# Attention and mixture of experts on one core: the scattered rows of six of the eight batches take a way through DRAM, the root of the variance moves ahead of the weights' low halves, and batch 0's scatters lose their pacing

## The chip, the core and the metric

The kernel runs on one core of a Trainium2 chip. The metric is the device time of one execution in microseconds (us). A core has five instruction streams that run side by side and wait for each other through semaphores: TensorE (PE in the profile; PEld is its loading of weights), VectorE (DVE), ScalarE (ACT), GpSimd (POOL) and SyncE (SP, which only issues transfers here). ACT and POOL issue transfers too. Sixteen DMA engines move the data.

## The reference

4096 tokens of 256 values, in 8 batches of 512. Each row is normalised, and two branches start from the normalised rows `xn`:

```
xn  = (x - mean) / sqrt(var + 1e-5)
# attention over channels, per batch
q, k, v = xn Wq, xn Wk, xn Wv
s   = softmax(q^T k / sqrt(8)) applied to v^T, transposed, times Wo
# mixture of experts, per token
scores  = softmax(xn gate^T)                 # 32 experts in 8 groups
chosen  = 6 best experts in the 3 best groups, weights normalised to 1
routed  = sum over chosen of weight_e * (silu(xn w1_e^T) * (xn w3_e^T)) w2_e^T
shared  = (silu(xn sw1^T) * (xn sw3^T)) sw2^T
out = x + s * silu(routed + shared)
```

## The kernel before

**Two phases.** The first goes over the 8 batches (B = 8). A batch is 4 tiles of 128 rows (TB = 4). For each it computes the attention branch (by the Gram matrix `xn^T xn`), the shared expert, the gate's scores, the choice of experts and the place of every row in a list sorted by expert, and it scatters the rows. The second phase takes the sorted list as 112 pairs of pages of 128 rows (PAIRS), runs the experts over them, stores the results into the same list, gathers 6 rows for each token, adds them up with their weights and writes the output.

**The list.** `slots_d` in DRAM, one row of 1 KB per (token, chosen expert). Its pages are first filled with zeros ("pads"): SP writes those that batch b can reach in `s_pads[b]` (4 smaller ones for batch 0, `s_first_pads[t]`), 3 MB each. Before the rows are scattered they are split in a high and a low half-precision half. ACT writes the high halves (`split_high`, L539), DVE the low ones (`split_low`, L995, semaphore `s_split`). The result is `split[b % 2]`, a ring of two tiles of one batch each, one in `early`, one in `work`.

**The scatters.** POOL scatters batch b with 24 indirect DMAs (4 tiles of rows, 6 chosen experts each; L487) of 128 rows. It needs the places (`s_slots`, DVE L989 at the end of `place`), the pads and the split rows. Their landing is counted in `s_disp[b % 2]`, and `split_high(b)` waits for the count of batch b - 2, as both use one tile. Ahead of some scatters POOL also waits for a count of PE's work (`let_pass`, L466 to L482): in each batch b ahead of scatter 2 for the gate's scores of batch b + 1 (`s_lg_ps`), ahead of 4 for the first half of the shared output (`s_y_ps`), 7 for the attention's product with Wo (`s_r_ps`), 9 for the second half (`s_y_ps`), 11 for the product with Wv (`s_m_ps`), 13 for the counts of rows per expert (`s_cnt`), 15 for the attention's output (`s_at_ps`), and 17, 19 and 21 for work of batch b + 1 (`s_ab_ps`, `s_a_ps`, and `s_xt_ps`, the transposes of batch b + 2 where there is one). No data needs these waits.

**The other streams in batch b.** Each runs its order as written out in `batch(b)`. PE: shared expert up, two products of the attention, transposes and gate of b + 1, softmax times Wo (L710), second half of the shared output (L726), product with Wv (L710), Gram matrix of b + 1 (L732), counts (L704, L705), attention output (L726). ACT: copies PSUM to SBUF between those; of note, after the shared output's copies and the store of `ysh_d` (L604) it normalises the first half of batch b + 2 (`normal`, L527), then copies the product with Wv (L610), then normalises the second half. `normal` needs `shift` and `rstd` from DVE. DVE: softmax's maximum, `spread_of(b + 2)` (mean and variance), `route(b + 1)` (choice of experts), `split_low(b + 1)`, `low_weights(b - 1)` (low halves of four experts' weights, 12 instructions of L1050), `spread_root(b + 2)` and `moved_mean` (L887 to L898, which give `rstd` and `shift`), `place(b + 1)`, `weigh(b + 1)`. The standard deviation that `spread_root` starts from was computed on ACT (L519) earlier in the batch.

**SP.** It loads x, loads of the batches ahead interleaved with the pads, each ahead of a wait for the choice of experts of an earlier batch (`s_sel`). Then it loads the last weights (L376), and then the pairs' rows (L403, L407), stores of results, and so on. The first 14 pairs (EARLY) may be loaded before all rows are scattered: `full_pairs` on DVE finds which pages no later batch can still reach after batch 6; SP loads those once the scatters of batches 0 to 6 have landed.

Of the kernel before, what the change touches and what calls it, by code (L numbers as in the profile page):

```python
# [7 lines left out]
ALU = mybir.AluOpType  # L8
# [43 lines left out]
EARLY = 14  # L52
# [41 lines left out]
def gated_attention_moe(nc, x, wq, wk_, wvT, wo, gwT, wexp, sw13T, sw2T, out):  # L94
    with ExitStack() as ctx:
# [12 lines left out]
        ysh_d = nc.dram_tensor("ysh_d", [T, H], F32).ap()  # L108

        x_b, ysh_b = (a.rearrange("(b t p) c -> b p t c", t=TB, p=P) for a in (x, ysh_d))  # L110
        x_t, ysh_t, out_t = (a.rearrange("(t p) c -> t p c", p=P) for a in (x, ysh_d, out))
# [42 lines left out]
        split = [v.rearrange("p (t c) -> p t c", t=TB) for v in (split_0, part(4608, 1024))]  # L154
        split16 = [v.bitcast(F16).rearrange("p (t s c) -> p t s c", t=TB, s=2) for v in (split_0, part(4608, 1024))]
# [113 lines left out]
        s_disp = sems("s_disp", XN_RING)  # L269
# [70 lines left out]
        def _(sp):  # L340
# [18 lines left out]
            for b in range(1, B):  # L359
                to = (b + 1) * BATCH_ROWS + E  # L360
                if b >= 2:
                    sp.wait_ge(s_sel, b - 1)
                if 3 <= b + 1 < B:
                    load_x(b + 1)
                sp.dma_start(slots_d[at * P:to * P].rearrange("(n p) c -> p n c", p=P),
                             pad[:].unsqueeze(1).to_broadcast([P, to - at, H])).then_inc(s_pads[b], 16)
                at = to

# [9 lines left out]
            sp.wait_ge(s_disp[0], 16 * BATCH_ROWS * (B // 2))  # L378
            sp.wait_ge(s_disp[1], 16 * BATCH_ROWS * (B // 2 - 1))
# [64 lines left out]
        def _(pool):  # L444
# [30 lines left out]

            for b in range(B):
# [14 lines left out]
            for k in range(XN_RING):  # L491
                pool.wait_ge(s_disp[k], 16 * BATCH_ROWS * (B // XN_RING))
# [21 lines left out]
        def _(act):  # L514
# [20 lines left out]
            def split_high(b):  # L535
                act.wait_ge(s_xn, b * TB + TB)
                if b >= XN_RING:
                    act.wait_ge(s_disp[b % XN_RING], 16 * BATCH_ROWS * (b // XN_RING))
                act.activation(split16[b % XN_RING][:, :, 0, :], xn[b % XN_RING], ACT.Copy, scale=X_UP).then_inc(s_split_hi, 1)  # L539
# [30 lines left out]
            def batch(b):  # L570
# [33 lines left out]
                act.dma_start(ysh_b[b], y_s).then_inc(s_ysh[b % 2], 16)  # L604
                if last:
# [259 lines left out]
        def _(dve):  # L865
# [126 lines left out]
            def split_low(b, tiles=range(TB)):  # L992
                dve.wait_ge(s_split_hi, b + 1)
                for t in tiles:
                    dve.scalar_tensor_tensor(split16[b % XN_RING][:, t, 1, :], xn[b % XN_RING][:, t], X_UP,  # L995
                                             split16[b % XN_RING][:, t, 0, :], ALU.mult, ALU.subtract).then_inc(s_split, 1)
# [67 lines left out]
            def batch(b):  # L1064
# [10 lines left out]
                elif b + 2 == B:  # L1075
# [125 lines left out]
```

## Time and profile before

| | |
|---|---|
| median of 3 runs | 686.68 us (683.47 to 690.63) |
| profiled execution, its own time | 691.99 us |
| its span, first to last instruction | 690.2 us |
| mean granted TensorE clock | 0.922 of full speed |
| PE busy | 548.6 us, 79% |
| POOL busy | 383.4 us, 56% |
| scatters (L487) | 192, from 28.7 to 317.7 us |
| gathers (L508) | 192, the first at 369.8 us |

The time outside of the span is 1.8 us. A busy share says how long an engine had an instruction in work; whether its idle time matters is read from who waits for it. In a row of the timeline the bracket says how long the engine was idle before the instruction and what released it: an instruction of another engine, "issue" (nothing that the profile shows), or "remote" (a semaphore whose sender the profile does not name). The ends of matmuls are modelled, so a signal that reaches its receivers long after the matmul's end is seen only from the receivers' rows.

### The profile page before, as it was taken

The numbers are of one execution on the slowest core, as the hardware profiler recorded it, in microseconds if no ns is written. First come the engines' busy times: TensorE is split into PE (matmuls) and PEld (weight loads), VectorE is DVE, ScalarE is ACT, GpSimd is POOL, SyncE is SP. The second block draws the span as 40 slices with busy tenths as digits, with TensorE's granted clock in tenths as the row PEclk, the third lists the DMA queues.
The fourth block names the chain that finished last, engine by engine and source line by source line (L and its number), as shares of the span: only waits on it lengthen the run. The fifth ranks groups of instructions, "written<-read, shape, count | busy, mean of one in ns | idle before, by whom it ended". The sixth has DMA issues, their size and how long they took to land.

```text
span 690.2 us, 14473 instructions
## 1 busy us (share of the span) xinstructions
PE 548.6 (79%) x4095; PEld 446.7 (65%) x4095; DVE 472.2 (68%) x1443; ACT 359.1 (52%) x606; POOL 383.4 (56%) x402
## 2 busy tenths in 40 slices
PE   7789696979697978437999889888888889888830
PEld 6566575756576765326999777777777777677620
DVE  6968687877788877722454567667677667667765
ACT  5546464546464644224655656556556556556421
POOL 1156667676666766753003556556565556565662
PEclk9889798998898999868999999999999999999975
DMA  9999996858393532754888888888888988888764
GB/s 320 416 354 347 366 334 227 285 214 298 130 334 113 207 117 91 230 150 122 201 217 262 290 280 283 280 280 285 290 272 292 279 279 267 290 276 286 226 198 141
DMA packets 111288, 174.80 MB, mean 253 GB/s; under 512 B 25072, under 2 KB 68848, under 8 KB 110320
## 3 DMA queue, kind: packets, MB, share of 16 engines
q1 hardware_dynamic: 87280, 108.29, 47.4%
q0 software_dynamic: 18432, 50.36, 23.2%
q10 hardware_dynamic: 5504, 15.24, 6.4%
q8 instruction: 40, 0.66, 0.4%
q14 instruction: 32, 0.26, 0.1%
HBM read 78.41 MB, written 92.27 MB: 247 GB/s over the span
## 4 chain that ended last, share of the span: by engine, by line
PE 53%; DVE 21%; issue 15%; another core or an unknown queue 6%; ACT 4%; DMA 1%; DVEq 0%; SPq 0%; ACTq 0%
PE ps L835 17%; PE ps L857 8%; PE ps L726 7%; PE ps L710 6%; PE ps L818 6%; PE ps L718 4%; DVE sw L1133 3%; PE ps L845 3%; PE ps L732 2%; DVE w_all L1050 2%; DVE work L1152 2%; DVE work L1159 1%; DVE stats L877 1%; DVE early L1141 1%
## 5 line engine op out<-in xcount | busy, mean ns | idle before, releaser
L508 POOL DMA_INDIRECT early<-slots_d,slot_at x192 | 186.6, 972 | 178.0 <-DMA slots_d<-early 56.6
L487 POOL DMA_INDIRECT slots_d<-early,slot_at x96 | 96.9, 1009 | 75.0 <-issue 25.7
L487 POOL DMA_INDIRECT slots_d<-work,slot_at x96 | 97.7, 1018 | 45.1 <-issue 26.5
L835 PE MATMUL ps<-w_all,xnT 128*128 x798 | 102.9, 275 | 15.9 <-issue 13.6
L835 PEld LDWEIGHTS ps<-w_all,xnT 128*128 128x128 f16 x798 | 71.4, 98 | 36.3 <-issue 24.6
L647 ACT ACTIVATE xnT<-ps 128x1024 f16<-128x1024 f16 x67 | 68.8, 1029 | 46.6 <-PE ps L818 28.0
L668 ACT ACTIVATE early<-ps 128x512 f32<-128x512 f32 x112 | 67.3, 602 | 46.6 <-remote 30.8
L818 PE MATMUL ps<-ident,work 128*128 128x128 f16 x796 | 66.7, 222 | 24.9 <-issue 24.8
L1159 DVE CAST work<-ps 128x256 f16<-128x256 f32 x75 | 31.6, 422 | 75.0 <-remote 45.0
L1133 DVE SCALAR_TENSOR_TENSOR sw<-early,wk,sw 128x256 f32<-128x256 f32 x160 | 77.7, 486 | 3.5
L818 PEld LDWEIGHTS ps<-ident,work 128*128 128x128 f16 x796 | 54.6, 99 | 28.8 <-issue 26.4
L653 ACT ACTIVATE work<-ps 128x256 f32<-128x256 f32 x112 | 43.9, 393 | 55.6 <-remote 37.9
L857 PE MATMUL ps<-w_all,work 128*128 x447 | 62.6, 277 | 0.9 <-issue 0.9
L1152 DVE SCALAR_TENSOR_TENSOR work<-ps,work 128x256 f32<-128x256 f32 x112 | 46.5, 416 | 20.4 <-ACT work L653 19.0
L710 PE MATMUL ps<-early,work 128*128 128x256 f32 x128 | 39.4, 462 | 25.8 <-ACT work L533 18.9
L835 PE MATMUL ps<-w_all,sw 128*128 x396 | 50.6, 274 | 8.3 <-issue 8.0
L710 PEld LDWEIGHTS ps<-early,work 128*128 128x128 f32 x128 | 28.6, 231 | 34.7 <-ACT work L533 21.0
L726 PE MATMUL ps<-work,early 128*128 128x256 f32 x128 | 34.7, 432 | 17.7 <-issue 13.8
L857 PEld LDWEIGHTS ps<-w_all,work 128*128 128x128 f16 x447 | 43.9, 99 | 6.3 <-issue 1.5
L835 PEld LDWEIGHTS ps<-w_all,sw 128*128 128x128 f16 x396 | 35.4, 98 | 18.6 <-issue 12.7
L647 ACT ACTIVATE sw<-ps 128x1024 f16<-128x1024 f16 x33 | 34.0, 1032 | 20.9 <-remote 15.4
L718 PE MATMUL ps<-xnT,sw 128*128 128x512 f16 x192 | 44.0, 379 | 0.0
(164 smaller groups left out, 989.4 us busy)
## 6 DMA issues: line engine op xcount, KB each, us to landing
slots_d<-early SPq DMA_DIRECT2D x112, 256.0 KB
work<-slots_d SPq DMA_DIRECT2D x100, 256.0 KB
slots_d<-pad SPq DMA_DIRECT2D x7, 3072.0 KB
w_all<-in_wexp ACTq DMA_DIRECT2D x7, 1536.0 KB
slots_d<-work SPq DMA_DIRECT2D x1, 5120.0 KB, 19.2
s_all<-in_x SPq DMA_DIRECT2D x8, 512.0 KB, 6.3
ysh_d<-work ACTq DMA_DIRECT2D x8, 512.0 KB
early<-ysh_d SPq DMA_DIRECT2D x32, 128.0 KB
```

Of the source, the lines that this page charges most:

```text
L487: pool.indirect_dma_start(slots_d[:, :], bass.IndirectOffsetOnAxis(ap=slot_at[:, at:at + 1], axis=0), split[b % XN_RING][:, t, :], None).t ...
L508: pool.indirect_dma_start(gath[:, at % GATH_RING, :], None, slots_d[:, :], bass.IndirectOffsetOnAxis(ap=slot_at[:, rank_of(at):rank_of(at) ...
L647: act.activation(x_halves[n % 3], turned_pair(p), ACT.Copy).then_inc(s_eT, 1)
L668: act.activation(y_e[:, p % DEEP, :], ps[:, 2 + p % 2, :], ACT.Copy, scale=1.0 / W_UP).then_inc(s_ey, 1)
L710: mm = pe.matmul(ps[:, bank, m * H:(m + 1) * H], lhs[:, k, m * P:(m + 1) * P], rhs[:, k, :], start=(k == 0), stop=(k == HC - 1))
L718: mm = pe.matmul(ps[:, 4 + 2 * m + w, :], sw13[:, w_low, w, k, m * P:(m + 1) * P], xnT16[:, x_low, k, :], start=(n == 0 and k == 0), stop= ...
L726: mm = pe.matmul(ps[:, bank + n, t * H:(t + 1) * H], lhs[:, k, at:at + P], rhs[:, k, :], start=(k == 0), stop=(k == HC - 1))
L818: mm = pe.transpose(turned_pair(p)[:, at:at + P], slot16[:, at_slot(p) + h, low, c * P:(c + 1) * P], ident16[:])
L835: mm = pe.matmul(ps[:, 5 + p % 2, h * 2 * I:(h + 1) * 2 * I], turned_x(p)[:, x_low * HC + k, h * P:(h + 1) * P], w16[:, bass.ds(at + (w_lo ...
L857: mm = pe.matmul(ps[:, 2 + p % 2, h * H:(h + 1) * H], hT_e[p % 3][:, h_low, h, :], w16[:, bass.ds(at + (w_low * WEXP + HC * 2 * I), H)], s ...
L1133: dve.scalar_tensor_tensor(acc[:, k, :], gath[:, at % GATH_RING, :], wk[:, rank_of(at):rank_of(at) + 1], ysh_l[k] if at % TOP_K == 0 else ...
L1152: dve.scalar_tensor_tensor(h_e[p % 2], up(p)[:, :, 1, :], 1.0 / (X_UP * W_UP), silu_e[p % 2], ALU.mult, ALU.mult).then_inc(s_eh, 1)
```

## The change

- **Rows through DRAM.** `split` gets a tile per batch: batch 0's is `passing`, the 4 KB per partition in `work`, those of batches 1 to 7 are all one tile in `early`. For batches 1 to 6 ACT stores the split rows to a new DRAM tensor `rows_d` (after the store of `ysh_d`), SP loads them tile by tile into `passing` as soon as that tile's scatters of the batch before have landed, and POOL scatters from `passing`. Batch 0 is scattered from `passing` directly, batch 7 from its own tile in `early`. `s_disp` is now counted per tile of rows, 4 semaphores in place of 2. `split_high(b)` waits for the store of batch b - 1 in place of the scatters of batch b - 2.
- **SP's order.** x of batches 3 and 4 ahead of the pads of batch 1, then per batch: the next x, the pads, the four loads of `passing`. The waits for `s_sel` are gone; what holds SP back is `s_rows` and `s_disp`.
- **Batch 0's scatters** wait for no count of PE's work.
- **DVE's order.** `spread_root(b + 2)` and `moved_mean` ahead of `low_weights(b - 1)`.
- **Early pairs.** Found after batch 5 in place of 6, 22 pairs in place of 14; SP may load them once batches 0 to 5 have landed.

```diff
-EARLY = 14
+EARLY, EARLY_BATCHES = 22, 6
...
-        split = [v.rearrange("p (t c) -> p t c", t=TB) for v in (split_0, part(4608, 1024))]
...
+        passing = part(4608, 1024, TB)
+        split_at = [part(4608, 1024)] + [split_0] * (B - 1)
+        split = [v.rearrange("p (t c) -> p t c", t=TB) for v in split_at]
...
             for b in range(1, B):
                 to = (b + 1) * BATCH_ROWS + E
-                if b >= 2:
-                    sp.wait_ge(s_sel, b - 1)
-                if 3 <= b + 1 < B:
-                    load_x(b + 1)
+                for n in (3, 4) if b == 1 else (b + 3,):
+                    if n < B:
+                        load_x(n)
                 sp.dma_start(slots_d[at * P:to * P].rearrange("(n p) c -> p n c", p=P),
                              pad[:].unsqueeze(1).to_broadcast([P, to - at, H])).then_inc(s_pads[b], 16)
                 at = to
+                if b < B - 1:
+                    sp.wait_ge(s_rows[b], 16)
+                    for t in range(TB):
+                        sp.wait_ge(s_disp[t], 16 * TOP_K * b)
+                        sp.dma_start(passing[:, t, :], rows_t[b * TB + t]).then_inc(s_passing[t], 16)
...
-            sp.wait_ge(s_disp[0], 16 * BATCH_ROWS * (B // 2))
-            sp.wait_ge(s_disp[1], 16 * BATCH_ROWS * (B // 2 - 1))
+            for t in range(TB):
+                sp.wait_ge(s_disp[t], 16 * TOP_K * EARLY_BATCHES)
...
-                if n in due:
+                if b >= 1 and n in due:
                     pool.wait_ge(*due[n])
...
-                    pool.wait_ge(s_split, b * TB + t + 1)
+                    if b == 0 or b == B - 1:
+                        pool.wait_ge(s_split, b * TB + t + 1)
+                    else:
+                        pool.wait_ge(s_passing[t], 16 * b)
...
                         pool.indirect_dma_start(slots_d[:, :], bass.IndirectOffsetOnAxis(ap=slot_at[:, at:at + 1], axis=0),
-                                                split[b % XN_RING][:, t, :], None).then_inc(s_disp[b % XN_RING], 16)
+                                                passing[:, t, :] if b < B - 1 else split[b][:, t, :], None
+                                                ).then_inc(s_disp[t], 16)
...
-                if b >= XN_RING:
-                    act.wait_ge(s_disp[b % XN_RING], 16 * BATCH_ROWS * (b // XN_RING))
+                if b >= 2:
+                    act.wait_ge(s_rows[b - 1], 16)
...
                 act.dma_start(ysh_b[b], y_s).then_inc(s_ysh[b % 2], 16)
+                if b + 2 < B:
+                    act.wait_ge(s_split, (b + 2) * TB)
+                    act.dma_start(rows_b[b + 1], split[b + 1]).then_inc(s_rows[b + 1], 16)
...
-                elif b + 2 == B:
+                if b + 1 == EARLY_BATCHES:
                     full_pairs()
...
                 split_low(b + 1)
-                if b >= 1:
-                    low_weights(b - 1)
                 if b + 2 < B:
                     spread_root(b + 2)
                     moved_mean()
+                if b >= 1:
+                    low_weights(b - 1)
                 place(b + 1)
```

POOL, the first scatters of batch 0 (the waits are for PE's gate of batch 1, shared output and product with Wo). Before:

```order
L487 DMA slots_d<-early,slot_at 28672x256 [waits s_first_pads0,s_split,s_slots]
L487 DMA slots_d<-early,slot_at 28672x256
L487 DMA slots_d<-early,slot_at 28672x256 [waits s_lg_ps]
L487 DMA slots_d<-early,slot_at 28672x256
L487 DMA slots_d<-early,slot_at 28672x256 [waits s_y_ps]
L487 DMA slots_d<-early,slot_at 28672x256
L487 DMA slots_d<-early,slot_at 28672x256 [waits s_first_pads1,s_split]
L487 DMA slots_d<-early,slot_at 28672x256 [waits s_r_ps]
L487 DMA slots_d<-early,slot_at 28672x256
L487 DMA slots_d<-early,slot_at 28672x256 [waits s_y_ps]
```

And now:

```order
L498 DMA slots_d<-work,slot_at 28672x256 [waits s_first_pads0,s_split,s_slots]
L498 DMA slots_d<-work,slot_at 28672x256 x5
L498 DMA slots_d<-work,slot_at 28672x256 [waits s_first_pads1,s_split]
L498 DMA slots_d<-work,slot_at 28672x256 x5
L498 DMA slots_d<-work,slot_at 28672x256 [waits s_first_pads2,s_split]
L498 DMA slots_d<-work,slot_at 28672x256 x5
```

Of the waits only those for the pads and for the split rows of a tile stay; in batch 0 the ten waits of `let_pass` are gone, and the source is in `work`.

DVE, in batch 2, from the low halves of batch 3's rows to the counts. Before:

```order
L995 SCALAR_TENSOR_TENSOR work<-early,work 128x256 [waits s_split_hi]
L995 SCALAR_TENSOR_TENSOR work<-early,work 128x256 x3
L1050 SCALAR_TENSOR_TENSOR w_all<-w_all 128x256 [waits s_whi]
L1050 SCALAR_TENSOR_TENSOR w_all<-w_all 128x256 x11
L887 RECIPROCAL rough<-std 128x4 [waits s_std]
L888 SCALAR_TENSOR_TENSOR newt<-rough 128x4 [waits s_chain]
L889 SCALAR_TENSOR_TENSOR newt<-mv,newt 128x4 [waits s_chain]
L890 SCALAR_TENSOR_TENSOR rstd<-newt,rough 128x4 [waits s_chain]
L898 SCALAR_TENSOR_TENSOR shift<-mv,rstd 128x4 [waits s_chain]
L947 MEMSET early 128x32
L949 COPY counts<-ps 128x4x32 [waits s_cnt]
```

And now (L1010 is the low halves, L1065 the weights', L902 to L913 root and shift, L964 the counts):

```order
L1010 SCALAR_TENSOR_TENSOR early<-early 128x256 [waits s_split_hi]
L1010 SCALAR_TENSOR_TENSOR early<-early 128x256 x3
L902 RECIPROCAL rough<-std 128x4 [waits s_std]
L903 SCALAR_TENSOR_TENSOR newt<-rough 128x4 [waits s_chain]
L904 SCALAR_TENSOR_TENSOR newt<-mv,newt 128x4 [waits s_chain]
L905 SCALAR_TENSOR_TENSOR rstd<-newt,rough 128x4 [waits s_chain]
L913 SCALAR_TENSOR_TENSOR shift<-mv,rstd 128x4 [waits s_chain]
L1065 SCALAR_TENSOR_TENSOR w_all<-w_all 128x256 [waits s_whi]
L1065 SCALAR_TENSOR_TENSOR w_all<-w_all 128x256 x11
L962 MEMSET early 128x32
L964 COPY counts<-ps 128x4x32 [waits s_cnt]
```

The five small instructions that give `shift` come ahead of the twelve for the weights.

SP, from the pads of batch 1 to the x that goes with batch 3. Before:

```order
L365 DMA slots_d<-pad 128x24x256 [waits s_const]
L342 DMA s_all<-in_x 128x4x256 [waits s_sel]
L365 DMA slots_d<-pad 128x24x256
L342 DMA s_all<-in_x 128x4x256 [waits s_sel]
L365 DMA slots_d<-pad 128x24x256
L342 DMA s_all<-in_x 128x4x256 [waits s_sel]
```

And now:

```order
L346 DMA s_all<-in_x 128x4x256 [waits s_const]
L346 DMA s_all<-in_x 128x4x256
L368 DMA slots_d<-pad 128x24x256
L375 DMA work<-rows_d 128x256 [waits s_disp0,s_rows1]
L375 DMA work<-rows_d 128x256 [waits s_disp1]
L375 DMA work<-rows_d 128x256 [waits s_disp2]
L375 DMA work<-rows_d 128x256 [waits s_disp3]
L346 DMA s_all<-in_x 128x4x256
L368 DMA slots_d<-pad 128x24x256
L375 DMA work<-rows_d 128x256 [waits s_disp0,s_rows2]
```

The pads of batch 2 stand behind four loads that wait for batch 0's scatters, and those of batch 3 behind the loads that wait for batch 1's.

## Rows read from the trace of the kernel before

**Rows 1.** Windows from POOL's first scatter of a batch to the next's: length, busy times, clock, DMA.
```profile
28.70:68.50 39.80, 33.83 (x151) 26.95 (x152) 32.01 (x119) 21.32 (x37) 23.88 (x24) 0.86 1.03 358
...
246.00:281.00 35.00, 28.44 (x114) 21.15 (x115) 27.47 (x98) 15.32 (x24) 24.13 (x24) 0.90 0.39 137
```
**Rows 2.** Timeline of POOL: scatters of batches 0, 1 and 2.
```profile
28.69 1.42 POOL L487 DMA_INDIRECT slots_d<-early,slot_at  x1 [25.64 <-DVE slot_at L989]
...
68.52 0.96 POOL L487 DMA_INDIRECT slots_d<-work,slot_at  x1 [0.30 <-issue]
...
79.16 1.73 POOL L487 DMA_INDIRECT slots_d<-work,slot_at  x1 [1.96 <-remote]
...
100.19 0.96 POOL L487 DMA_INDIRECT slots_d<-work,slot_at  x1 [1.27 <-PE ps L685]
...
103.98 0.96 POOL L487 DMA_INDIRECT slots_d<-early,slot_at  x1 [0.30 <-issue]
```
**Rows 3.** Timeline of DVE: places of batch 1; low weights, shift of batch 5.
```profile
58.80 0.18 DVE L989 TENSOR_TENSOR slot_at<-in_order,in_page 128x24 int32<-128x24 int32 x1
...
147.00 4.10 DVE L1050 SCALAR_TENSOR_TENSOR w_all<-w_all 128x256 f16<-128x256 f32 x12
...
154.04 0.16 DVE L898 SCALAR_TENSOR_TENSOR shift<-mv,rstd 128x4 f32<-128x4 f32 x1 [0.54 <-DVE rstd L890]
```
**Rows 4.** Timeline of PE: product with Wv in batch 1; attention output, batches 3 and 4.
```profile
73.32 1.89 PE L726 MATMUL ps<-early,work 128*128 128x256 f32 x8
79.56 3.78 PE L710 MATMUL ps<-work,early 128*128 128x256 f32 x8 [4.36 <-issue]
...
156.84 6.74 PE L726 MATMUL ps<-work,early 128*128 128x256 f32 x16 [3.61 <-ACT work L610]
...
194.19 3.72 PE L726 MATMUL ps<-work,early 128*128 128x256 f32 x16 [0.26 <-ACT work L610]
```
**Rows 5.** Timeline of ACT: batch 0, then the signals that came late, batches 1 to 7.
```profile
43.98 0.60 ACT L602 ACTIVATE work<-ps 128x512 f32<-128x512 f32 x1 [2.15 <-PE ps L710]
...
46.34 0.38 ACTq L604 DMA_DIRECT2D ysh_d<-work  x1
...
47.84 0.57 ACT L610 ACTIVATE work<-ps 128x512 f32<-128x512 f32 x1
...
78.91 0.60 ACT L602 ACTIVATE work<-ps 128x512 f32<-128x512 f32 x1 [3.87 <-remote]
...
156.19 0.60 ACT L610 ACTIVATE work<-ps 128x512 f32<-128x512 f32 x1 [0.36 <-remote]
...
292.00 0.60 ACT L598 ACTIVATE work<-ps 128x512 f32<-128x512 f32 x1 [10.13 <-remote]
```
**Rows 6.** Waits, by length: first 320 to 369 us, then 375 to 650 us.
```profile
DVE work L1159 <- PE ps L845: 16.6, 14, 1.9
...
DVE work L1159 <- remote: 42.6, 23, 4.0
```
**Rows 7.** Timeline of POOL: the last two waits ahead of the one at 292 us.
```profile
272.08 0.96 POOL L487 DMA_INDIRECT slots_d<-early,slot_at  x1 [1.84 <-remote]
...
298.07 0.95 POOL L487 DMA_INDIRECT slots_d<-work,slot_at  x1 [3.38 <-remote]
```
**Rows 8.** DMA issues: KB each, us to landing; 60 to 130 us, then whole span.
```profile
s_all<-in_x SPq DMA_DIRECT2D x2, 512.0 KB, 10.1
...
s_all<-in_x SPq DMA_DIRECT2D x8, 512.0 KB, 6.3
...
slots_d<-work SPq DMA_DIRECT2D x2, 512.0 KB, 19.8
```
**Rows 9.** Timeline of PE: last attention output, then the first pair of pages.
```profile
298.48 5.90 PE L726 MATMUL ps<-work,early 128*128 128x256 f32 x16 [13.80 <-issue]
...
312.21 1.86 PE L818 MATMUL ps<-ident,work 128*128 128x128 f16 x16 [7.72 <-issue]
```

More of the change, by code:

```diff
@@ L108, in gated_attention_moe @@
         ysh_d = nc.dram_tensor("ysh_d", [T, H], F32).ap()
-        x_b, ysh_b = (a.rearrange("(b t p) c -> b p t c", t=TB, p=P) for a in (x, ysh_d))
-        x_t, ysh_t, out_t = (a.rearrange("(t p) c -> t p c", p=P) for a in (x, ysh_d, out))
+        rows_d = nc.dram_tensor("rows_d", [T, H], F32).ap()
+        x_b, ysh_b, rows_b = (a.rearrange("(b t p) c -> b p t c", t=TB, p=P) for a in (x, ysh_d, rows_d))
+        x_t, ysh_t, out_t, rows_t = (a.rearrange("(t p) c -> t p c", p=P) for a in (x, ysh_d, out, rows_d))
         w_all = sb("w_all", [P, E * WEXP])
@@ L153, in gated_attention_moe @@
         y_s = part(3584, 1024, TB)
-        split = [v.rearrange("p (t c) -> p t c", t=TB) for v in (split_0, part(4608, 1024))]
-        split16 = [v.bitcast(F16).rearrange("p (t s c) -> p t s c", t=TB, s=2) for v in (split_0, part(4608, 1024))]
+        passing = part(4608, 1024, TB)
+        split_at = [part(4608, 1024)] + [split_0] * (B - 1)
+        split = [v.rearrange("p (t c) -> p t c", t=TB) for v in split_at]
+        split16 = [v.bitcast(F16).rearrange("p (t s c) -> p t s c", t=TB, s=2) for v in split_at]
         mx, nmx, rsum, rinv = (sb(n, [P, HC]) for n in ("mx", "nmx", "rsum", "rinv"))
@@ L268, in gated_attention_moe @@
         s_split_hi, s_split = sem("s_split_hi"), sem("s_split")
-        s_disp = sems("s_disp", XN_RING)
+        s_disp = sems("s_disp", TB)
+        s_rows, s_passing = sems("s_rows", B), sems("s_passing", TB)
         s_g_ps, s_a_ps, s_s_ps, s_r_ps, s_m_ps = (sem(f"s_{n}_ps") for n in "gasrm")
@@ L487, in _ @@
                         pool.indirect_dma_start(slots_d[:, :], bass.IndirectOffsetOnAxis(ap=slot_at[:, at:at + 1], axis=0),
-                                                split[b % XN_RING][:, t, :], None).then_inc(s_disp[b % XN_RING], 16)
-            for k in range(XN_RING):
-                pool.wait_ge(s_disp[k], 16 * BATCH_ROWS * (B // XN_RING))
+                                                passing[:, t, :] if b < B - 1 else split[b][:, t, :], None
+                                                ).then_inc(s_disp[t], 16)
+            for t in range(TB):
+                pool.wait_ge(s_disp[t], 16 * TOP_K * B)
             pool.sem_inc(s_scattered, 1)
@@ L536, in split_high @@
                 act.wait_ge(s_xn, b * TB + TB)
-                if b >= XN_RING:
-                    act.wait_ge(s_disp[b % XN_RING], 16 * BATCH_ROWS * (b // XN_RING))
-                act.activation(split16[b % XN_RING][:, :, 0, :], xn[b % XN_RING], ACT.Copy, scale=X_UP).then_inc(s_split_hi, 1)
+                if b >= 2:
+                    act.wait_ge(s_rows[b - 1], 16)
+                act.activation(split16[b][:, :, 0, :], xn[b % XN_RING], ACT.Copy, scale=X_UP).then_inc(s_split_hi, 1)
             def turned(b):
@@ L994, in split_low @@
                 for t in tiles:
-                    dve.scalar_tensor_tensor(split16[b % XN_RING][:, t, 1, :], xn[b % XN_RING][:, t], X_UP,
-                                             split16[b % XN_RING][:, t, 0, :], ALU.mult, ALU.subtract).then_inc(s_split, 1)
+                    dve.scalar_tensor_tensor(split16[b][:, t, 1, :], xn[b % XN_RING][:, t], X_UP,
+                                             split16[b][:, t, 0, :], ALU.mult, ALU.subtract).then_inc(s_split, 1)
             def weigh(b):
```

## The prediction

> **What bounds the kernel now.** I read first the windows by batch [rows 1]: POOL's scatters of one batch take 39.8 us for batch 0 and 35 for batch 6, of which POOL is busy 24. In neither is an engine full: PE is busy 33.8 and 28.4 us. So the batches are paced by waits between engines, and I read the timelines of POOL, PE and ACT against each other. Batch 0's scatters run from 28.69 to 68.52 us, batch 1's to 103.98 [rows 2]; the last end at 317.7. 24 scatters back to back would take 24 x 1.27 = 30.4 us (0.96 each and 0.30 between them, as in these rows), so batch 0 contains 9.4 us of waits for PE's counts.
>
> POOL's waits are no mere loss. In batch 1 PE began L726 at 73.32, so the product with Wo ahead of it was through by about then [rows 4], but ACT received that product's signal at 78.91, after 3.87 us from "remote" [rows 5]. POOL, which had scattered without a break and then stopped at its own wait for the same signal, went on at 79.16 after 1.96 us [rows 2]. The same shows at 156.19 [rows 5], at 272.08 and at 298.07 [rows 7]: PE's signals arrive some 1.6 to 3 us after POOL has stopped. Where POOL issues nothing (320 to 369 us) DVE's wait at L1159 is put down to PE, 14 times; with gathers running it is "remote" 23 times for 42.6 us [rows 6]. I call such a signal held. A held signal costs PE twice: it stalls (4.36 us, 3.61 us) and then runs its next matmuls slower (3.78 us for eight of a kind that take 1.89 just before; 6.74 for sixteen that take 3.72 in the next batch) [rows 4], the granted clock of these windows being 0.86 to 0.90 [rows 1]. The second phase starts when PE has ended the last attention output and read its table (7.72 us) [rows 9]; it runs from 312.2 us to the end and is not changed. **What moves 312.2 is what moves the time.**
>
> **Batch 0 without waits: -9.4 us for POOL, at most.** Its scatters would end at 28.7 + 30.4 = 59.1. Batch 1 may start then, since its places are written at 58.98 [rows 3]. Batch 1 keeps its waits for PE: the one ahead of scatter 21 let go at 100.19, 1.27 us after POOL came to it, on PE's transposes [rows 2]. Were PE's times unchanged, POOL would get through batch 1 only 1.3 us earlier. But now POOL would be the one that waits, and a POOL that waits holds nothing: the 4.36 us stall in batch 1 and the 1.9 us lost in the product behind it (3.78 against 1.89) [rows 4] go, 6.3 us. 1.3 + 6.3 = **-7.6 us** at the start of batch 2. From there on POOL trails PE much as before, since its 30.4 us are as long as PE's batch.
>
> **Held signals in batch 0: +4.5 us.** Without waits POOL issues for 30 us on end while PE runs batch 0. The signal of the product with Wo reached ACT at 43.98 [rows 5], 15 us after POOL's first scatter. The held signal of batch 1 was due when POOL had scattered without a stop for 5 us and more (from before 68.52), that at the end for 10 (from 272.08 to 281.9, where ACT's wait began) [rows 2, 5, 7]. So I expect it to be held. How long has one precedent: at the end, POOL stopped at 272.08 and next at 298.07 [rows 7], and ACT got a signal from PE at 292.00, 10.13 us late [rows 5], so 20 us after the stop. In batch 0 that is 28.7 + 20 = 48.7, or 4.7 us later than 43.98; I take 4.5. The ends: nothing, if the signals pass as they did in that batch; and 13.1 us, if they are held until POOL has ended (59.1 + 1.8 = 60.9, against L610 at 47.84 [rows 5]). I take the precedent as the row most like it. The delay moves batch 1's places by the same amount and so takes its share of the -7.6.
> The Trainium skill says otherwise ("SBUF — State Buffer", the section on what contends): PE and ACT have their own ports and wait on nobody, only DVE and GpSimd share a pair. By that nothing in batch 0 is held and the sum would be 4.5 us better. This case's trace speaks against relying on it: 23 waits that appear with POOL's transfers, none without [rows 6].
>
> **Variance's root ahead of the low halves: -3 us.** `shift` of batch 5 came at 154.04, behind 4.10 us of L1050 [rows 3]. ACT's copy L610 stands behind the `normal` that needs it and began at 156.19, PE stalled 3.61 us and then took 6.74 for sixteen matmuls, 3.0 more than in batch 4 [rows 4]: 6.6 us. Half of that is also explained by the held signal (0.36 us "remote" at L610 even after `normal`) [rows 5]. Ends: 0 and 6.6; I take 3. In the other batches the copy or its product was late anyway. The low halves lose nothing: DVE waited for PE's counts behind them.
>
> **The way through DRAM: +0.5 us.** Six stores of 512 KB and 24 loads of 128 KB. ACT issues each store in 0.38 us, as the one of `ysh_d` [rows 5], 2.3 us in all ahead of `normal`; where ACT waits for `shift` that is hidden, so I take 0.5 (ends 0 and 2.3). The wait for `s_split` ahead of it is covered: the low halves end some 4 us before that place in each batch. The store of batch 1's rows would be issued at about 46.8, right behind the one at 46.34 [rows 5], so the round trip has 12.3 us until 59.1. Rows for it: a load of 512 KB lands in 6.3 us in the median, 10.1 in the loaded stretch, 19.8 for pads behind other pads [rows 8]. Twice 6.3 is 12.6: it just fits. Batch 0 and 1 have their engines of DMA full now (share 1.03 [rows 1]), but the pads of batch 2, issued at 40 us now, move behind batch 0's scatters, and the queue is empty when the rows pass.
> The Trainium skill ("DMA: Bandwidth & Descriptors", anatomy of one DMA) gives about 2 us fixed per transfer, mostly for the receipt of the write, longest into HBM, plus bytes at 436 GB/s. The estimate by that page is 3.2 + 2.3 = 5.5 us for the round trip, under what I allow; no row here shows such a transfer alone.
> x of batches 3 and 4 come earlier, nobody waits. `passing` of a tile is free 18 scatters before it is needed. SP's new waits end with batch 5's scatters, and the last weights behind them are asked for at 275 us: nothing. 22 early pairs and a count after batch 5: PE asks for its first pair at 312.21 after reading its table [rows 9], with the loads there: nothing.
>
> **Sum.** -7.6 + 4.5 - 3.0 + 0.5 = -5.6 us. The profiled execution took 692.0, so it would take 686.4; against the median of 686.7 it is **681.1 us**. The profiled one stood 5.3 us above that median, a spread which is part of the range.
>
> **Rivals.**
> 1. *Nothing is held in batch 0, and more stalls fall away.* -7.6 - 6.6 = -14 us, and should POOL trail PE less at the end, also part of the 13.8 us for which PE stood at 298.48 [rows 9]: 673 down to 664. For: ACT's signals of batch 0 come on time now. Against: POOL stops in it every few scatters now. Chance 0.25.
> 2. *Batch 0's signals are held until POOL ends.* L610 comes 13.1 us later, batch 1's places at 72, start 3.6 us later than 68.5; batch 1 then runs without its stall, and the root gives its 3. PE is 13.1 late and regains 6.3 + 3.0; with the 0.5 that is +4.3: 691. For: every long run of scatters has a held signal. Chance 0.22.
> 3. *The rows come late* (the slower side). The place is POOL's first scatter of batch 1. With 19.8 us for the store and 6.3 for the load the rows are there at 46.8 + 26.1 = 72.9, 4.4 us after 68.5; it decides from 21.7 us on. POOL's later start delays nothing of PE in batch 1, but if the same holds in batches 2 and 3 (DMA share 0.7 to 1) POOL falls a further 4 us back in each and its stops, and with them PE's signals, move: +4 to +12, 691 to 699. Against: 6.3 and 10.1 for x. Chance 0.13.
> My own case has 0.40, with 676 to 686 for it.
>
> **How the numbers follow.** From case 1's middle to case 3's: 666 to 693 leaves out about 2 in 10. A measurement of this kernel tells 1% from no change, 6.9 us: faster is under 679.8. My case lies on both sides of that (0.17 of its 0.40 under it); with case 1 that is 0.42 faster. Same: 0.23 of my case, 0.15 of case 2: 0.38. Slower, over 693.5: the rest of cases 2 and 3, and what I have not seen, 0.20.
>
> **What the profile after would show.** The last of batch 0's scatters near 59 us, and batch 1's first one within 1 us of it (case 3: a wait of several us for `passing`; case 2: for `slot_at` until about 72). ACT's copies L602 and L610 in batch 0 at 48 and 52, "remote". PE's stall after batch 1's product with Wo under 1 us. Batch 2's first scatter at 96 to 102. ACT's wait for `shift` in batches 3 to 5 gone. PE's first pair of pages at 306. Wrong would be all of it if the second phase, from there to the end, took other than its 378 us.

## The result: slower by 1.6%, and the profile after

The changed kernel takes 699.48 us in the median of 4 runs (696.95 to 700.77), the kernel before 688.65 beside it (4 runs, 683.47 to 692.09): a ratio of 1.0158, 95% interval 1.0111 to 1.0205. The forecast was 681.1 us, range 666 to 693. The profiled execution took 698.92 us with a span of 697.2, 6.9 us more than the one before, where the medians differ by 10.8; the traces account for the 6.9 alone. The ratios here and below are formed from the single runs, not from the two medians (they differ by up to 0.006), and leave out one run of 2213.7 us of e2 and one of 1092.59 us of e20.

The second phase begins, in the timeline of PE after, 7.2 us later than before:

```profile
50.83 0.22 PE L720 MATMUL ps<-sel,tri 128*128 128x128 bf16 x1
63.39 5.81 PE L741 MATMUL ps<-work,early 128*128 128x256 f32 x16 [12.34 <-ACT work L625]
...
88.22 1.89 PE L741 MATMUL ps<-early,work 128*128 128x256 f32 x8
89.95 1.89 PE L725 MATMUL ps<-work,early 128*128 128x256 f32 x8
...
130.40 6.43 PE L741 MATMUL ps<-work,early 128*128 128x256 f32 x16 [4.28 <-issue]
...
156.28 3.72 PE L725 MATMUL ps<-early,work 128*128 128x256 f32 x8 [6.43 <-ACT work L545]
...
166.86 3.67 PE L741 MATMUL ps<-work,early 128*128 128x256 f32 x16
...
191.23 3.78 PE L725 MATMUL ps<-early,work 128*128 128x256 f32 x8 [7.68 <-ACT work L545]
...
319.41 1.87 PE L833 MATMUL ps<-ident,work 128*128 128x128 f16 x16 [7.55 <-issue]
```

Against 312.21 [rows 9]. The phase then lasts 377.8 us, before 378.0: nothing changed in it. So the loss lies in the first phase, and the first row that departs from before is the second one, in batch 0. PE had done the counts at 51 us and stood for 12.34 us, for ACT's copy of the product with Wv. ACT's timeline has the two signals that it got late, behind one that came on time:

```profile
44.07 0.60 ACT L614 ACTIVATE work<-ps 128x512 f32<-128x512 f32 x1 [2.30 <-PE ps L725]
49.41 0.60 ACT L610 ACTIVATE work<-ps 128x512 f32<-128x512 f32 x1 [4.74 <-remote]
50.03 0.38 ACTq L616 DMA_DIRECT2D ysh_d<-work  x1
50.45 1.26 ACTq L619 DMA_DIRECT2D rows_d<-early  x1
...
62.74 0.60 ACT L625 ACTIVATE work<-ps 128x512 f32<-128x512 f32 x1 [9.81 <-remote]
```

The product with Wo (L602 before, L614 now) is copied as before, at 44.07 against 43.98 [rows 5]. The second half of the shared output (L598 before, L610 now) was copied just ahead of the store at 46.34 [rows 5] and now is at 49.41, after 4.74 us. The product with Wv (L610 before, L625 now) was at 47.84 [rows 5] and is at 62.74, 14.9 us later. DVE, waiting for the counts, got the same release:

```profile
62.97 0.39 DVE L964 COPY counts<-ps 128x128 f32<-128x128 f32 x1 [13.34 <-remote]
...
70.54 0.18 DVE L1004 TENSOR_TENSOR slot_at<-in_order,in_page 128x24 int32<-128x24 int32 x1
```

and so the places of batch 1 are there at 70.54 in place of 58.80 [rows 3]. POOL, in its timeline:

```profile
28.62 1.42 POOL L498 DMA_INDIRECT slots_d<-work,slot_at  x1 [25.56 <-DVE slot_at L1004]
...
58.53 0.96 POOL L498 DMA_INDIRECT slots_d<-work,slot_at  x1 [0.30 <-issue]
71.00 1.02 POOL L498 DMA_INDIRECT slots_d<-work,slot_at  x1 [11.51 <-DVE slot_at L1004]
...
80.69 0.96 POOL L498 DMA_INDIRECT slots_d<-work,slot_at  x1 [7.21 <-PE ps L713]
```

POOL did what the forecast said: batch 0 in one go, the last scatter at 58.53, through by 59.5 (59.1 was forecast). Then it stood idle for 11.51 us, until the places were there. The last signals reached ACT and DVE at 62.7 to 63.0, 3.3 to 3.5 us after POOL had ended; the one at 49.41 came while POOL went on issuing. The windows by batch, as in [rows 1], show the price in the clock too:

```profile
28.62:71.00 42.38, 25.36 (x92) 20.24 (x93) 24.04 (x94) 12.81 (x24) 23.86 (x24) 0.72 0.92 324
```

PE is busy 25.36 us of 42.38 at a clock of 0.72, where it was 33.83 of 39.80 at 0.86 [rows 1].

How PE stands against before, read where it begins the transposes at the head of each batch:

| transposes in batch | before, us | after, us | difference |
|---|---|---|---|
| 1 | 61.22 | 75.94 | +14.7 |
| 2 | 97.79 | 105.66 | +7.9 |
| 3 | 132.50 | 143.57 | +11.1 |
| 4 | 170.32 | 177.27 | +7.0 |
| 5 | 204.65 | 213.50 | +8.9 |
| 6 | 237.53 | 248.57 | +11.0 |
| first pair of pages | 312.21 | 319.41 | +7.2 |

Batch 1 gives back 6.8: the product with Wv at 89.95 begins right behind the row ahead of it and takes 1.89 us, where it was 4.36 of stall and 3.78 [rows 4], 6.3 us in all. Batch 3 gives back 4.1, though the product with Wo at 156.28 stood for 6.43 us: the attention output at 166.86 has no stall and takes 3.67, where it was 3.61 and 6.74 [rows 4]. Batch 2 loses 3.2 (4.28 us of stall at 130.40), and batches 4 and 5 lose 1.9 and 2.1 (stalls of 7.68 us at 191.23 and of 7.43 at 227.22; the same product, the one with Wo, stood for 6.44 and 4.69 before).

By the traces these losses are held signals too; no run takes them away by themselves. In batch 2 ACT waits for the second half of the shared output, and copies the product with Wv (L625) 24.1 us after the batch's transposes, before 20.9:

```profile
126.23 0.60 ACT L610 ACTIVATE work<-ps 128x512 f32<-128x512 f32 x1 [6.49 <-remote]
```

In batches 4 and 5 it is the gate's scores, which DVE reads first in L940:

```profile
187.81 0.29 DVE L940 TENSOR_REDUCE row<-ps 128x4 f32<-128x128 f32 x1 [3.10 <-remote]
...
223.80 0.29 DVE L940 TENSOR_REDUCE row<-ps 128x4 f32<-128x128 f32 x1 [4.21 <-remote]
```

PE ends the gate 4.5 us after its transposes in both batches and both kernels. The scores reach DVE 10.5 and 10.3 us after the transposes, before 9.3 and 7.6, and PE's stall grows by just that (1.24 and 2.74 us): softmax's weights on ACT (L545), for which the product with Wo stands, come behind DVE's work on the scores. Each of these three signals arrives within 0.3 us of the end of a "remote" wait of POOL (126.48, 188.05 and 224.04). DVE waited for the scores before as well (3.11 and 2.08 us); the signals now come later against PE.

### The profile page after: what moved, and what is told of

It is laid out like the page before. It is cut to its first block, busy times and chain, and to the rows that moved or that the text cites. A ratio compares the mean times of both kernels' runs of the same rounds, so it can differ in the third digit from the quotient of the medians.

```text
span 697.2 us, 14519 instructions
## 1 busy us (share of the span) xinstructions
PE 549.9 (79%) x4095; PEld 446.9 (64%) x4095; DVE 471.9 (68%) x1443; ACT 359.3 (52%) x606; POOL 380.9 (55%) x402
## 4 chain that ended last, share of the span: by engine, by line
PE 55%; DVE 18%; issue 12%; another core or an unknown queue 8%; ACT 3%; DMA 1%; POOL 1%; ACTq 0%; POOLq 0%; DVEq 0%
PE ps L850 20%; PE ps L872 9%; PE ps L833 6%; PE ps L725 5%; PE ps L741 5%; PE ps L860 3%; PE ps L733 3%; PE ps L747 2%; DVE sw L1148 2%; DVE w_all L1065 1%; DVE work L1167 1%; DVE stats L892 1%; PE ps L713 1%; DVE work L1174 1%
## 5 line engine op out<-in xcount | busy, mean ns | idle before, releaser
L498 POOL DMA_INDIRECT slots_d<-work,slot_at x168 | 167.3, 996 | 119.4 <-issue 48.5
L668 ACT ACTIVATE work<-ps 128x256 f32<-128x256 f32 x112 | 43.8, 392 | 62.7 <-PE ps L850 43.1
L725 PE MATMUL ps<-early,work 128*128 128x256 f32 x128 | 41.4, 481 | 33.3 <-ACT work L545 26.0
L725 PEld LDWEIGHTS ps<-early,work 128*128 128x128 f32 x128 | 30.1, 243 | 42.6 <-ACT work L545 28.0
L741 PE MATMUL ps<-work,early 128*128 128x256 f32 x128 | 37.9, 462 | 24.1 <-ACT work L625 12.3
L741 PEld LDWEIGHTS ps<-work,early 128*128 128x128 f32 x128 | 29.7, 239 | 30.5 <-issue 12.8
L860 PE MATMUL ps<-ident,work 128*128 128x128 f32 x223 | 44.4, 277 | 4.5 <-issue 3.0
```

The source lines that it names most:

```text
L498: pool.indirect_dma_start(slots_d[:, :], bass.IndirectOffsetOnAxis(ap=slot_at[:, at:at + 1], axis=0), passing[:, t, :] if b < B - 1 else s ...
L725: mm = pe.matmul(ps[:, bank, m * H:(m + 1) * H], lhs[:, k, m * P:(m + 1) * P], rhs[:, k, :], start=(k == 0), stop=(k == HC - 1))
L741: mm = pe.matmul(ps[:, bank + n, t * H:(t + 1) * H], lhs[:, k, at:at + P], rhs[:, k, :], start=(k == 0), stop=(k == HC - 1))
L860: mm = pe.transpose(turned_hidden(p)[:, h * P:(h + 1) * P], h_e[p % 2][:, h, :], ident[:])
```

## The experiments

**Two conditions.** The same kernel before was measured at 688 to 691 us in some sessions on the chips and at 589 to 591 in others. In the trace of a 589 us run of it (e9, a single run) no wait is put down to "remote"; in the one of 692 us there are 117 such waits for 249 us. Of all the traces here nine have 95 to 127 of them and the other eleven none. I call these conditions *free* and *held*. The result above is from the held one. It isn't a fixed property of a chip: one chip was free in one session and held in a later one. What decides it, I don't know. So no run is compared with one of the other condition; each ratio below is to the kernel before on the same chip in the same session.

| run | kernel | this / before, us | ratio, 95% interval |
|---|---|---|---|
| *held:* the change | | 699.48 / 688.65 | 1.0158 (1.0111 to 1.0205) |
| e13_before_free0 | before, batch 0's waits taken away | 696.56 / 687.89 | 1.0126 (1.0058 to 1.0194) |
| e20_paced0 | the change, batch 0's waits put back | 689.95 / 691.31 | 0.9995 (0.9962 to 1.0028) |
| e19_paced0_five | the change, five of the ten put back | 692.66 / 691.31 | 1.0015 (0.9977 to 1.0054) |
| e11_paced0_pairs14 | as e20, 14 early pairs | 690.49 / 689.66 | 0.9995 (0.9961 to 1.0029) |
| e14_own_stops | the change, POOL stops in batch 0 for its own scatters | 696.30 / 687.89 | 1.0118 (1.0053 to 1.0183) |
| e15_free_all | the change, no waits of `let_pass` in any batch | 789.01 / 687.89 | 1.1409 (1.1309 to 1.1509) |
| e16_before_root | before, root ahead of the low halves | 688.63 / 687.89 | 0.9988 (0.9957 to 1.0019) |
| *free:* e5_after | the change | 581.58 / 590.22 | 0.9856 (0.9832 to 0.9880) |
| e6_free_all | as e15 | 581.43 / 590.22 | 0.9857 (0.9831 to 0.9883) |
| e1_paced0 | as e20 | 582.57 / 589.47 | 0.9884 (0.9861 to 0.9908) |
| e7_paced0_again | as e20 | 582.73 / 590.22 | 0.9871 (0.9842 to 0.9899) |
| e10_paced0_third | as e20 | 582.69 / 590.65 | 0.9861 (0.9831 to 0.9891) |
| e2_before_free0 | as e13 | 590.32 / 589.47 | 1.0020 (1.0002 to 1.0038) |
| e8_before_free0_again | as e13 | 589.13 / 590.22 | 0.9985 (0.9963 to 1.0008) |
| e3_before_root | as e16 | 591.21 / 589.47 | 1.0038 (1.0019 to 1.0057) |
| e12_before_root_free0 | before, with both edits | 588.00 / 589.51 | 0.9968 (0.9951 to 0.9984) |
| e4_dram_alone | the change without root and free batch 0 | 589.70 / 589.47 | 1.0001 (0.9980 to 1.0023) |

**Batch 0's waits alone.** Put back in the changed kernel, or taken out of the kernel before:

```diff
-                if b >= 1 and n in due:
+                if n in due:                  # e1, e7, e10, e20; e2, e8, e13 the reverse in before
```

e1 expected: 

> The changed kernel with batch 0's ten waits for PE's counts put back. Theory H (a signal of PE is held while POOL issues scatters without a stop, and that is what the change lost): ACT's copy of the product with Wv in batch 0 begins near 48 us as before, not at 62.7, places of batch 1 at 59, start of the second phase 8 to 13 us earlier than the changed kernel's 319; ratio to before 0.985 to 1.003. Theory D (the way through DRAM and SP's order cost the time): it stays at 1.01 to 1.02.

e2 expected: 

> The kernel before with batch 0's ten waits taken away and nothing else. Theory H: ACT's copy of the product with Wv in batch 0 waits some 10 us for a remote signal and begins at 61 to 63 us; ratio to before 1.010 to 1.020. Theory D: batch 1's scatters start at 59 us, 9 us earlier, and the ratio is 0.985 to 1.000.

Both of these, and their repeats e7, e8 and e10, fell in the free condition and could say nothing on held signals (e1's ratio is inside its range for held signals, but by another gain, that of the root with the way through DRAM, below): there the waits cost and give next to nothing (1.0020 and 0.9985; the three measurements of the paced kernel and the change lie within 0.3% of each other). The same two kernels later met the held condition.

e13 expected: 

> The kernel before with batch 0's ten waits taken away, nothing else. Where signals are held (kernel before at 685 to 692 us): theory H 1.010 to 1.022, ACT's copy of the product with Wv in batch 0 at 60 to 63 us, so that part of the change alone gives the loss; rival (the waits' absence hurts only with the way through DRAM): 0.995 to 1.005. Where they are not held: 0.998 to 1.004 again.

e20 expected: 

> The changed kernel with all ten waits of batch 0 back, 22 early pairs. Where signals are held: as the same with 14 early pairs, 0.994 to 1.004, second phase from 308 to 313 us. Rival (22 early pairs are part of the loss there): 1.008 to 1.018. Where they are not held: 0.986 to 0.989 again.

e13 loses 1.3% from this edit alone; e20 has lost nothing. In e13's timeline of ACT the row of 62.74 is there again, without the way through DRAM and without the moved root:

```profile
62.88 0.60 ACT L610 ACTIVATE work<-ps 128x512 f32<-128x512 f32 x1 [11.14 <-remote]
```

Its second phase begins at 319.37 us (after: 319.41), that of e20 at 311.72 (before: 312.21). So batch 0's waits are the whole loss, as far as these runs tell (to 0.3%).

**Which of the waits?** With those ahead of scatters 7, 9, 11, 15 and 21 put back, five of ten:

```diff
-                if b >= 1 and n in due:
+                if n in due and (b >= 1 or n in (7, 9, 11, 15, 21)):
```

Expected: 

> The changed kernel with five of batch 0's ten waits for PE back: ahead of scatters 7, 9, 11, 15 and 21, the places where POOL stopped for its own scatters in the run before. Where signals are held: theory H, the product with Wv is copied at 48 to 50 us in batch 0 and POOL ends the batch by 66 to 68, since a wait for PE that is due costs POOL 1 to 3 us where one for its own landing cost 2 to 6; ratio 0.990 to 1.003. Rival (POOL needs all ten): 1.005 to 1.020. Where they are not held: 0.984 to 0.990.

1.0015 with an interval that takes in 1: these five are enough. The product with Wv is copied at 48.64.

**Must POOL wait for PE, or only stop?** In e14 POOL stops in batch 0 at the same five places, but for the landing of its own last scatter:

```diff
                     pool.wait_ge(*due[n])
+                elif b == 0 and n in (7, 9, 11, 15, 21):
+                    pool.wait_ge(s_disp[(n - 1) // TOP_K], 16 * ((n - 1) % TOP_K + 1))
```

Expected: 

> The changed kernel, where POOL in batch 0 waits for no count of PE, but at scatters 7, 9, 11, 15 and 21 for the landing of its own scatter just before, so it stops without asking PE for anything. Theory H (what lets PE's signals pass is that POOL stops): where signals are held, ACT's copy of the product with Wv in batch 0 at 48 to 53 us, ratio 0.990 to 1.006. Rival (it is the wait on PE's own semaphore that matters): copy at 58 to 63 us, 1.010 to 1.022. Where they are not held: as the changed kernel, 0.984 to 0.990.

Its timelines of ACT and of POOL:

```profile
49.11 0.58 ACT L627 ACTIVATE work<-ps 128x512 f32<-128x512 f32 x1
```
```profile
43.50 0.96 POOL L500 DMA_INDIRECT slots_d<-work,slot_at  x1 [5.58 <-DMA slots_d<-work,slot_at]
...
51.59 1.08 POOL L500 DMA_INDIRECT slots_d<-work,slot_at  x1 [5.71 <-DMA slots_d<-work,slot_at]
...
77.31 1.04 POOL L500 DMA_INDIRECT slots_d<-work,slot_at  x1 [0.30 <-issue]
```

The copy has no wait at all, so PE's signals pass at this stop of POOL too, which asks PE for nothing. They pass while POOL's last scatter is still on its way (the stop ends with its landing, at 51.59): scatters in flight alone did not hold them. DVE has the counts at 50.98, PE ended them at 50.94. But the five stops last 18.2 us (5.58, 5.71, 2.75, 2.44, 1.70), where the ten for PE take 9.4 in all before: POOL comes to batch 1 at 77.31, before at 68.52 [rows 2]. The ratio is 1.0118, where 0.990 to 1.006 was expected. The second phase of the profiled execution begins only 2.4 us late (314.62), and that execution took 693.1 us, 3.2 under the median of its kernel; so the ratio is measured, its split between POOL's lost time and the rest is not.

**No waits at all.**

```diff
-                if b >= 1 and n in due:
+                if False and n in due:
```

Held (e15) expected: 

> The changed kernel with none of let_pass's waits in any batch. Where signals are held: theory H 1.03 to 1.10, with one or more waits of about 10 us for remote in every batch. Rival (only batch 0, whose scatters meet the heaviest transfers, matters): 1.010 to 1.022, as the changed kernel. Where they are not held: 0.984 to 0.990 again.

Free (e6) expected: 

> The changed kernel with none of let_pass's waits, in no batch. Theory H (POOL issuing without a stop holds PE's signals): where signals are held at all, POOL's batches run back to back and PE's are held for up to 10 us and more several times a batch: ratio to before 1.02 to 1.08. Where they are not held: 0.975 to 0.995, near the changed kernel. The rival, that the waits merely cost POOL time: faster than the changed kernel by 1 to 3% in either.

One kernel, 1.1409 held, well over both expected ranges, and 0.9857 free. In e15's timeline of POOL each batch is now as batch 0 was after:

```profile
71.23 1.02 POOL L498 DMA_INDIRECT slots_d<-work,slot_at  x1 [11.64 <-DVE slot_at L1004]
...
121.45 1.02 POOL L498 DMA_INDIRECT slots_d<-work,slot_at  x1 [19.92 <-DVE slot_at L1004]
```

A batch takes 44.9 to 51.2 us from batch 1 on (starts at 71.23, 121.45, 171.14, 222.31, 270.06, 315.01), and the copy of the product with Wv in batch 1 waits 9.77 us for "remote". The second phase begins at 410.97 us and lasts 376.7, so the loss lies in the first again. The let-pass waits, which no data needs, are worth some 100 us in this condition (789.01 against 687.89 for the kernel before).

**The root alone,** in the kernel before.

```diff
                 split_low(b + 1)
-                if b >= 1:
-                    low_weights(b - 1)
                 if b + 2 < B:
                     spread_root(b + 2)
                     moved_mean()
+                if b >= 1:
+                    low_weights(b - 1)
```

Free (e3) expected: 

> The kernel before with DVE's root and shift ahead of the low halves of the weights, nothing else. My sum gave it -3 us (0 to -6.6): ratio 0.990 to 1.000, no wait of ACT for shift in batches 1 to 5. The rival: the copy behind it was held anyway, no change, 0.998 to 1.003.

Held (e16) expected: 

> The kernel before with the root ahead of the low halves, nothing else. Where signals are held: my sum had -3 us (0 to -6.6), 0.990 to 1.000; rival, the copy behind it is held anyway, 0.998 to 1.003. Where they are not held: 1.002 to 1.006 again.

Neither gains: 1.0038, a small loss that neither side had expected, and 0.9988. The free traces show why for e3. Waits by length of the kernel before (e9), 20 to 320 us:

```profile
ACT early L527 <- DVE shift L898: 23.4, 6, 5.2
ACT work L539 <- DMA slots_d<-work,slot_at: 4.1, 2, 2.3
...
ACT early L539 <- DMA slots_d<-early,slot_at: 2.2, 2, 1.6
```

and of e3:

```profile
ACT work L539 <- DMA slots_d<-work,slot_at: 11.6, 3, 6.7
ACT early L539 <- DMA slots_d<-early,slot_at: 6.3, 3, 3.9
ACT early L527 <- DVE shift L898: 5.8, 3, 3.9
```

ACT's wait for `shift` shrinks from 23.4 to 5.8 us. What it wins, it stands at the next wait: the high halves (L539) go into the tile of batch b - 2, whose scatters haven't landed, 6.3 us before and 17.9 now. The ring of two tiles holds most of the gain back.

**The way through DRAM alone,** root and batch 0 as before (the two diffs above undone in the changed kernel).

Expected: 

> The changed kernel without its other two parts: batch 0's waits put back and the root behind the low halves again; what is left is the way through DRAM, SP's order and the early pairs. My sum gave it +0.5 us: ratio 0.997 to 1.004. Theory D: 1.01 to 1.02, with POOL waiting for rows that come late at the start of a batch or a tile. The difference to the kernel with the root moved is the root's worth there.

1.0001: nothing, as its waits for `shift` are still there. With the root it is 0.9861 to 0.9884 (e1, e7, e10). Neither edit gains by itself, both together do: the one takes away the wait that hides the other's. Root and free batch 0 with the old ring (e12) give 0.9968, a gain of 0.3%, with 12.9 us of ACT's waits for scatters: the ring is what holds the root's gain back, not batch 0.

e12 expected: 

> The kernel before with two parts of the change, the root ahead of the low halves and batch 0 free of waits, but with the ring of two tiles in place of the way through DRAM. Theory R (without held signals the root's gain of some 7 us needs the way through DRAM, since in the ring ACT's high halves wait for the scatters of two batches before): ratio 0.998 to 1.005, with 8 to 18 us of ACT's waits for scatters. Rival: it was batch 0's waits that the root lacked, 0.984 to 0.990. Where the kernel before takes 685 to 692 us: batch 0's signals held, 1.005 to 1.020.

**The change itself, free.**

e5 expected: 

> The changed kernel, unchanged, once more. The first four experiments ran at 589 us for the kernel before, with no wait put down to remote, where the first comparison had 688 us and 16 kinds of such waits; theory C says that the holding of PE's signals behind POOL's scatters is present in some of the measurements and absent in others, and that the change's sign hangs on it. Where the kernel before takes 685 to 692 us: ratio 1.011 to 1.021 again. Where it takes 589 us: 0.980 to 0.992, as the same kernel with batch 0 paced gave 0.988 there. A rival (the first comparison's loss has another cause than held signals): 1.01 to 1.02 in both.

A gain of 1.4%, and from the same kernel a loss of 1.6% held. The second phase begins at 262.89 (e9: 270.04). Here the round trip of the rows can be read. ACT's queue, SP's queue and POOL of e5:

```profile
47.48 1.32 ACTq L619 DMA_DIRECT2D rows_d<-early  x1
```
```profile
57.18 8.59 SPq L375 DMA_DIRECT2D work<-rows_d  x4
```
```profile
59.20 0.96 POOL L498 DMA_INDIRECT slots_d<-work,slot_at  x1 [0.30 <-issue]
66.42 0.95 POOL L498 DMA_INDIRECT slots_d<-work,slot_at  x1 [6.26 <-DMA work<-rows_d]
```

18.9 us pass from the store's issue to the scatter that was waiting for the first load, 9.7 until the first load is issued and 9.2 behind that. POOL stands for 6.26 us, and batch 1 begins at 66.42, in e9 at 66.44. This is my third rival's mechanism, and it takes POOL's lead. No measurement tells a cost of it: e5 and the paced e7 of the same session are 0.9856 and 0.9871. The lead is worth nothing without the way through DRAM either: in e8 batch 1 begins at 60.11, but POOL then stands for 4.40 us for PE's gate, and the ratio is 0.9985.

**The early pairs.**

```diff
-EARLY, EARLY_BATCHES = 22, 6
+EARLY, EARLY_BATCHES = 14, 6
```

Expected: 

> The changed kernel with batch 0's waits put back and 14 early pairs in place of 22 (still those known after batch 5). My sum gave the early pairs nothing: the same ratio as with 22, 0.986 to 0.989, where the kernel before takes 589 us. Rival: the larger number of early pairs is part of the gain, 0.990 to 1.000. Where the kernel before takes 685 to 692 us: theory H 0.985 to 1.003 and ACT's copy of the product with Wv in batch 0 near 48 us; the rival 1.01 to 1.02.

0.9995 as e20 with 22: no effect held; free it was not run.

## Why the prediction was wrong, by its own steps

**The step that failed is "Held signals in batch 0: +4.5 us".** It measures +14.9 at the copy of the product with Wv, which waits 9.81 us "remote" behind another wait of 4.74. The mechanism was named rightly; signal and size were not. I took the product with Wo for the held one, and that came on time (44.07, not my 48). And the size came from a precedent that I read too short. From [rows 7] and [rows 5] I took 20 us from POOL's stop at 272.08 to the signal at 292.00. That signal is only the first of two: ACT's timeline of before goes on with

```profile
297.83 0.60 ACT L610 ACTIVATE work<-ps 128x512 f32<-128x512 f32 x1 [3.22 <-remote]
```

and POOL's wait that ended at 298.07 lasted 3.38 us [rows 7], so the second signal came 3.1 us after POOL had stopped, and not sooner. Neither signal is the product with Wo's: they are the second half of the shared output (L598) and the product with Wv. Batch 0 of after is the same picture: the first held signal after 20.8 us of scatters (28.62 to 49.41), the second 3.3 us after POOL was through. The term had to be read at the second. Even my upper end was short by 1.8 us, as it put the release 1.8 us after POOL's end and it was 3.3 (and that end 0.4 us too early). e13 and e20 show that this term, with what it sets off in later batches, is the loss.

**POOL free in batch 0, -7.6.** Its larger half holds: PE's stall in batch 1 and the slow product behind it, put at 6.3 us, are gone, and the batch as a whole gave back 6.8. That it goes on from there as before did not hold: a held signal costs 3.2 us more in batch 2. The 1.3 of POOL's own lead never came, since POOL waited 11.51 us for its places. The rest of the step, that POOL ends at 59.1, was right to 0.4 us.

**The root, -3.** In place it did what it should: no wait for `shift` in batches 1 to 5 of after, and 4.1 us given back in batch 3. Over the kernel it is worth nothing that a measurement tells (e16: 0.9988, interval 0.9957 to 1.0019, so at most 3 us held). The 4.1 of batch 3 are lost again in batches 4 and 5, to the held scores of the gate; no run tries that by itself.

**The way through DRAM, +0.5.** Right in the total (e4, free: 1.0001; held it was run only with the root, e20: 0.9995), wrong on the way to it: I allowed 12.6 us for the round trip, and in e5 it is 18.9. In the held condition POOL's wait for its places covers it; free it eats POOL's lead. The estimate of 5.5 us by the Trainium skill ("DMA: Bandwidth & Descriptors", anatomy of one DMA) is further off; the page describes one transfer, issued by GpSimd, and here a store of ACT's and four loads of SP's ran beside scatters, at a DMA share of 0.80 over those 18.9 us (e5).

**The rule that PE and ACT wait on nobody** (the Trainium skill, "SBUF — State Buffer"): I kept it at a distance for the 23 "remote" waits of [rows 6]. The page speaks of the ports of SBUF, and what waits here are signals, so no run here contradicts the page; what fails is my reading of it as "nothing is held". Held, engines do wait (13.34 us of DVE and 9.81 of ACT, gone in e20); free, no row has such a wait. There the measured difference is -8.6 us, where my sum was -5.6 and the one by that reading -10.1; but it comes from the root with the way through DRAM, not from batch 0.

**The rivals.** The second was right: held until POOL ends, places of batch 1 at 72 (70.54), PE 13.1 late (14.9), its stall in batch 1 gone. It gave 691, +4.3 us, because it had PE's delay 1.8 us too small, let the root give its 3 us and let nothing be lost again in batches 2, 4 and 5. The steps of the table, 14.7 - 6.8 + 3.2 - 4.1 + 1.9 + 2.1 - 3.8 (what the stretch up to the first pair regains), are the 7.2 us by which the second phase begins later; that they add up is no proof of their causes. Its chance of 0.22 was too low: "for" had "every long run of scatters", and the only argument for my own case was the one precedent. Of the first rival only "nothing is held" is true, and only in the free condition, where no stall of that kind is there to fall away. The second phase took 377.8 of the 378 us forecast.

**The best version** of those run is the changed kernel with batch 0's waits put back: 0.9861 to 0.9884 free, 0.9995 held. Held it is better than the change (1.0158), free it stands within 0.3% of it; against the kernel before it gains only in the free condition.

**What stays open.** What puts a session in the held condition; by what mechanism a signal of PE is kept from ACT and DVE while POOL issues scatters (the traces show only "remote"), and why one sometimes passes in the middle of a run of them; and how much of e14's loss is POOL's lost time.

## What to carry to other kernels

Waits that no data needs may hold the kernel's time: before one is taken away, look for who gets signals while the waiting engine stands, and take it away alone (here five of ten were enough, and all of them worth 14%). A price read from a precedent must follow the whole chain to the row that the next engine waits for, not stop at its first signal. An edit that gains nothing by itself may free another one: try them in pairs before one is thrown out, and in as many sessions as can be had, since one kernel gave 0.986 in one and 1.016 in another.

## What the runs showed of the hardware that I had not expected

- One program, 589 and 689 us, according to the session. 60 of the 103 us between the two profiled spans are in the second phase (378.0 held, 317.6 free), where PE is busy 118.89 of 140 us between 400 and 540 in the one, and 140.00 in the other.
- Waits for signals of PE of up to 13.34 us while POOL issues indirect transfers back to back (PE had ended those counts 11.9 us before DVE began). Most come 1 to 3.5 us after POOL stops, whether it stops for PE, for its own transfers (e14) or at the end of its batch; a few come in the middle of a run (49.41 us after, 212.21 and 292.00 before).
- 18.9 us from the issue of a store of 512 KB to DRAM to the scatter that waits for the first 128 KB back, with other scatters beside them (e5).
